# Layer 0 of a four-layer network: the placing of a batch drawn together within the next attention, and four of nine expert weight pairs asked for at the end of the last attention

## The reference, cut to what matters

```python
# attention of layer 0: 16 heads of width 16, keys and values from ctx_1024
scores = jnp.einsum('bhqd,bhkd->bhqk', Q, K) / math.sqrt(DK)
scores = jnp.where(m == 0, jnp.float32(-1000000000.0), scores)
out = jnp.einsum('bhqk,bhkd->bhqd', jax.nn.softmax(scores, axis=-1), V)
...
# experts of layer 0: 64 experts, 8 for each token, 64 slots in each expert
probs = jax.nn.softmax(logits, axis=-1)
topk_p, topk_i = jax.lax.top_k(probs, TOP_K)
flat_e = topk_i.reshape(-1)
pos_all = jnp.cumsum(jax.nn.one_hot(flat_e, NUM_EXPERTS, dtype=jnp.int32), axis=0) - 1
pos = jnp.take_along_axis(pos_all, flat_e[:, None], axis=1)[:, 0]
dispatch = dispatch.at[flat_e, pos].set(x_rep, mode='drop')
g = jax.nn.silu(jnp.einsum('ech,eih->eci', dispatch, w_gate))
u = jnp.einsum('ech,eih->eci', dispatch, w_up)
y = jnp.einsum('eci,ehi->ech', g * u, w_down)
```

## Time and profile before

| what | value |
|---|---|
| median of 3 runs | 3057.17 us (3050.08 to 3061.91) |
| the profiled execution's own time | 3043.72 us |
| its span | 3042.0 us |
| granted TensorE clock over the span | 0.904 of full speed |
| PE, DVE, ACT, POOL busy | 82%, 60%, 38%, 26% of the span |
| instructions | 35373 |

### The profile page before, as it was taken

The page is one execution under the profiler, slowest core; times in us unless marked ns, Lnnn a source line. Parts: engine busy times, 40 slices in busy tenths (PEclk is TensorE's granted clock), DMA queues, the critical chain, the costliest instruction groups (busy, mean ns, idle before and its releaser), DMA issues. The chain is left out here.

```text
span 3042.0 us, 35373 instructions
## 1 busy us (share of the span) xinstructions
PE 2490.5 (82%) x12480; PEld 1337.2 (44%) x12480; DVE 1813.2 (60%) x4051; ACT 1169.4 (38%) x2095; POOL 788.1 (26%) x494
## 2 busy tenths in 40 slices
PE   6885865086687969979989988989998998997996
PEld 2332322032354534545554454555464555454554
DVE  5673742214787747357758447776736775835775
ACT  1432331022232415245635325654415653513662
POOL 1004124462000014114414204432303442401441
PEclk8997976588587879989999999999998999998998
DMA  7411000787420020034440024432012443002442
GB/s 230 121 35 16 15 14 14 220 258 253 153 76 7 8 98 1 8 108 114 106 109 29 8 85 104 113 97 75 8 70 77 118 111 97 1 19 90 114 119 75
DMA packets 113983, 257.07 MB, mean 85 GB/s; under 512 B 37222, under 2 KB 57318, under 8 KB 107786
## 3 DMA queue, kind: packets, MB, share of 16 engines
q1 hardware_dynamic: 93978, 220.26, 24.3%
q10 hardware_dynamic: 12656, 25.97, 3.4%
q0 software_dynamic: 7168, 8.50, 1.0%
HBM read 119.81 MB, written 29.74 MB: 49 GB/s over the span
## 5 line engine op out<-in xcount | busy, mean ns | idle before, releaser
L856 POOL TENSOR_SCALAR pbuf<-pbuf,recip 128x1024 f32<-128x1024 f32 x128 | 364.4, 2847 | 946.9 <-DVE recip L760 946.9
L805 ACT ACTIVATE pbuf<-ps,least 128x1024 f32<-128x1024 f32 x256 | 284.1, 1112 | 297.9 <-DVE least L753 215.4
L753 DVE CUSTOM_DVE_ANT_0 ps<-ps,mask 128x1024 f32<-128x1024 f32 x256 | 308.0, 1244 | 143.4 <-PE ps L685 142.3
L582 POOL TENSOR_SCALAR pbuf<-pbuf,recip 128x512 f32<-128x512 f32 x128 | 200.1, 1574 | 463.5 <-DVE recip L503 463.5
L685 PE MATMUL ps<-kH,qT 64*128 64x512 f32 x1024 | 267.3, 642 | 51.2 <-ACT pbuf L805 48.4
L710 PE MATMUL ps<-work,vh 128*64 128x256 f32 x2048 | 251.8, 390 | 0.0
L553 ACT ACTIVATE pbuf<-ps,least 128x512 f32<-128x512 f32 x256 | 172.5, 685 | 159.1 <-DVE least L493 159.1
L767 DVE STREAM_TRANSPOSE pbuf<-pbuf 128x2048 f32<-128x2048 f32 (+1 forms) x128 | 226.3, 1768 | 0.8 <-issue 0.8
L1501 ACT ACTIVATE early<-ps 128x1536 f32<-128x1536 f32 x86 | 123.9, 1440 | 258.2 <-PE ps L1334 196.6
L1574 DVE TENSOR_REDUCE mh<-ps 128x3 f32<-128x1536 f32 x86 | 150.0, 1744 | 104.0 <-PE ps L1323 59.6
L990 POOL DMA_INDIRECT slot_token<-info,place x128 | 127.1, 993 | 242.1 <-DVE info L1739 193.8
(11 more groups left out here) (343 smaller groups left out, 4073.7 us busy)
## 6 DMA issues: line engine op xcount, KB each, us to landing
work<-pbuf SPq DMA_DIRECT2D x784, 96.0 KB, 2.5
work<-pbuf ACTq DMA_DIRECT2D x240, 96.0 KB, 2.9
early<-in_L_wgu SPq DMA_DIRECT2D x22, 768.0 KB
expert_rows<-zero_rows SPq DMA_DIRECT2D x16, 1024.0 KB, 11.5
yg<-expert_rows SPq DMA_DIRECT2D x16, 1024.0 KB, 5.9
early<-in_L_wd SPq DMA_DIRECT2D x22, 384.0 KB
arena<-in_L_wo SPq DMA_DIRECT2D x8, 1024.0 KB, 9.0
arena<-in_L_wff SPq DMA_DIRECT2D x4, 2048.0 KB, 9.3
```

What stands on the lines that cost most here:

```text
L582: nc.gpsimd.tensor_scalar(x, x, recip[:, n % 8:n % 8 + 1], None, mult).then_inc(probs_ready[1], 1)
L753: nc.vector.tensor_tensor_reduce(out=x, in0=x, in1=mask, scale=1.0, scalar=FMAX, op0=add, op1=ALU.min, accum_out=least[:, n % 8:n % 8 + 1])\
L805: nc.scalar.activation(to, x, ACT.Exp, bias=least[:, n % 8:n % 8 + 1], scale=-1.0, accum_out=sums[:, n % 8:n % 8 + 1]).then_inc(taken, 1)
L856: nc.gpsimd.tensor_scalar(unit(n), unit(n), recip[:, n % 8:n % 8 + 1], None, mult).then_inc(pool_divided, 1)
```

## The change

It does three things. (1) The numbers at which the pieces of a batch's routing stand are drawn closer: from base + 31.6 to 48.8 before to base + 31.6 to 43.85; GpSimd's `hand_out`, which issues a burst, goes from base + 53 to base + 43. (2) SyncE issues the weights of four pairs (`AT_ONCE`) as soon as the attention's last product is made, ahead of the last batch's rows, and the other five when the last batch is placed. (3) A wait on `normed` is put ahead of the reciprocal in `divide`, for the instruction that read the same buffer before. No operation is added or left out otherwise.

```diff
+AT_ONCE = 4
...
-                at["back", b, i] = t + 31.6 + i
-                at["project", b, i] = t + 33.6 + i
-                at["rows", b, i] = t + 38.6 + i
-            at["logits", b, 0] = t + 40.6
-            at["place", b, 0] = t + 43.6
+                at["back", b, i] = t + 31.6 + 0.7 * i
+                at["project", b, i] = t + 33.1 + 0.7 * i
+                at["rows", b, i] = t + 37.4 + 0.6 * i
+            at["logits", b, 0] = t + 38.7
+            at["place", b, 0] = t + 40.7
...
+                    if b == B - 1:
+                        sp.wait_ge(av_done, BLOCKS // 4)
+                        for i in range(AT_ONCE):
+                            load_pair(sp, a, pair_weights(early, i), i, early_in[i])
                     sp.wait_ge(x1n_ready, b + 1)
...
-                sp.wait_ge(av_done, BLOCKS // 4)
                 sp.wait_ge(placed, 2 * B - 1)
-                for i in range(EARLY):
+                for i in range(AT_ONCE, EARLY):
                     load_pair(sp, a, pair_weights(early, i), i, early_in[i])
...
                 def hand_out(b):
-                    yield base[b] + 53
+                    yield base[b] + 43
...
+                        if b or g:
+                            v.wait_ge(normed, b * QUADS + g)
                         link(nc.vector.reciprocal(r16[:, :, :], o[:, :, :, DK0]))
...
                     for n, last in enumerate(layernorm_steps(nc, link, x1, x1n, stats)):
-                        yield t0 + 35.45 + n * 0.5
+                        yield t0 + 34.3 + n * 0.2
...
-                        yield t0 + 46.3 + 1.5 * half
+                        yield t0 + 42.1 + 1.05 * half
...
-                        yield t0 + 46.8 + 1.5 * half
+                        yield t0 + 42.45 + 1.05 * half
...
-                        yield t0 + 47.3 + 1.5 * half
+                        yield t0 + 42.8 + 1.05 * half
                         nc.vector.tensor_reduce(w8[:, some, :], junk[:, some], AX.X, add).then_inc(placed, 1)
```

More of the change, by code:

```diff
@@ L1532, in routed @@
                 def routed(b):
-                    yield base[b] + 41.6
+                    yield base[b] + 39.4
                     act.wait_ge(chosen, b + 1)
@@ L1676, in route @@
                     nc.vector.tensor_scalar(negm[:, :], m8[:, :, 0], -1.0, None, mult).then_inc(chosen, 1)
-                    yield t0 + 41.3
+                    yield t0 + 39.3
                     v.wait_ge(chosen, b + 1)
@@ L1681, in route @@
                     link(last)
-                    yield t0 + 41.9
+                    yield t0 + 39.6
                     link(nc.vector.tensor_tensor(sel[:, :, :], rep[:, :, :], lg[:, :, :], ALU.not_equal))
-                    yield t0 + 42.5
+                    yield t0 + 39.9
                     for t in range(NT):
@@ L1698, in route @@
                     last.then_inc(job_kept, 1)
-                    yield t0 + 44.3
+                    yield t0 + 41.2
                     nc.vector.tensor_copy(before[:, 0, :], before[:, NT, :])
@@ L1707, in route @@
                     link(last)
-                    yield t0 + 44.9
+                    yield t0 + 41.5
                     nc.vector.tensor_tensor(ex[:, :, :], ex[:, :, :], valid[:, :, :], mult)
                     link(nc.vector.tensor_tensor(key[:, :, :], key[:, :, :], valid[:, :, :], mult))
-                    yield t0 + 45.5
+                    yield t0 + 41.8
                     for t in range(NT):
```

## The result

The changed kernel takes 3081.45 us (median of 5 runs, 3075.54 to 3083.83) where the kernel before, on the same chip, takes 3054.91 (5 runs, 3050.08 to 3061.91). The ratio is 1.0076, with a 95% interval of 1.0052 to 1.0100. It is slower, by some 23 us. The forecast was +9 and 3066, so the time lies inside the range, on the side that had a chance of 0.31.

A forecast was written before the change was run, and what follows sets the result against it. Layer 0 was held bound by the attention's 3.0 us steps (VectorE search plus wait) and by scatter bursts stopping it, burst 4 being itself the path; +8 + 9 - 8 = +9 us on 3057.17 gave 3066, range 3034 to 3088.

The forecast's parts named there:

- the side that had a chance of 0.31: Whole kernel: slower than before by over 0.5%, meaning above 3072 us; chance 0.31.
- The slower rival: Attention: TensorE's jobs in bank 7 wait on VectorE's copies behind searches; +20, +11 and -4, 3084 us; chance 0.25.
- Drawn together, +8.: Routing of batches 0 to 2 in attention: same VectorE work meets fewer free gaps; +8 us, ends -10 and +20.
- Batch 1's thirteen steps above 60 us: Batch 1's routing in the attention: 50.6 us before; above 60 us would show the forecast wrong.
- Burst 3 moved, +9.: Burst 3 goes from the tail onto attention steps: costs 27 us instead of 17.5; +9 us, bounds 0 and +11.
- Bursts 1 and 2: 0.: Both bursts move 4.5 steps earlier and stay over attention, stopping the same kind of work; 0 us.
- The early weights, -8.: Burst 4 and start of experts: fewer weight loads beside the burst shorten its waits; -8 us, ends -4 and -14.
- of the others I take half of 6.9: Burst 4's other waits, among them 2.75 and 6.9 us: half of 6.9 us counted as saved.
- The tail is freed: End of attention: burst 3 costs little over the last steps and the tail's 17.5 us go; 3029 us; chance 0.20.
- Bursts do not stop engines: Bursts: another thing causes the still part, so moving burst 3 changes nothing; +8 + 0 - 8, 3057 us; chance 0.11.
- The moved bias add: GpSimd's last bias add waits up to 41 us longer behind burst 1, its reader over 200 us on; cost 0.
- the added wait on `normed`: Ahead of each reciprocal, for an instruction already behind VectorE in its own order; cost 0.

The follow-up runs named there:

- e_paced: The changed kernel with every second scatter of bursts 1 and 2 waiting for the exponents to go on; 3016.23 us, 0.9902 of before.
- e_last_two: The kernel before with the changed kernel's numbers for batches 2 and 3 alone, weights as before; 3065.41 us, 1.0067 of before.
- e_weights: The kernel before with the early weights alone, all numbers of the order as before; 3029.12 us, 0.9938 of before.
- e_after_again: The changed kernel run once more, unchanged, where the kernel before takes 3048.34 us; 3073.84 us, 1.0087 of before.
- e_eights: The changed kernel with bursts 1 and 2 cut into runs of eight scatters, five steps apart, on the second chip; 2979.22 us, 1.0091 of before.

## Why the prediction was right in sign and short in size

The measured time lies in the forecast's range, but its mechanism did not put it there. The three terms came to +25, +11 and -5 us in the trace where the forecast had +8, +9 and -8. The time lies at the edge of what the forecast calls its own bounds, -3 and +25 us (3082), which don't follow from the ends of its terms: these add up to -24 and +27. The slower rival stretched the range to 3088.

- **"Drawn together, +8."** This is the step that failed: the term of the sum with a cost left out. It measured +25.1 us in the trace, and +29.2 on the chip without the standstill, above even its own upper end of +20. The step counted lost gaps of 1.25 us on VectorE and took each step as the sum of its work. By the rows, what it left out is that work in one piece delays the search, that TensorE idles for it (4.56 us), and that it then runs at half speed for 9 us; 20.7 of the 25.1 us lie in the steps where that happens. That the clock, and not the drawing of the norm as such, makes them long was not tested. "No compute instruction is added", and still TensorE is busy 36.7 us instead of 28.9 in those eight steps, for 15 instructions more.
- **"Batch 1's thirteen steps above 60 us"** was named as what would prove it wrong, and so it was: without a standstill in them (`e_paced`) they take 67.7 us, where before's took 50.6.
- **"Burst 3 moved, +9."** Right in mechanism and close in size: +29.9 inside for -18.5 in the tail, 11.4 net, just above its upper bound of +11; 9.3 net in `e_last_two`. The forecast put 27 against 17.5. It began at 494.66, and less the 4.2 and 25.1 us of delay that is 465, where the forecast had it.
- **"Bursts 1 and 2: 0."** Roughly so. Compared with the spaced kernels of the second chip, the steps to exponent 49 from 38 cost 32.4 us more before and 25.0 in the changed kernel, those to exponent 70 from 57 30.8 and 34.3. That is 31 to 32 us a burst before, where the forecast had 28, and 4 us less together now; neither moved by over 8.
- **"The early weights, -8."** -5.0 in the changed kernel, inside its bounds. The term named its parts, and one of two came. SyncE's read now starts 1.2 us behind the last scatter instead of 6.9 (644.50 and 643.28). The other half of the gain, "of the others I take half of 6.9", didn't come; POOL's waits of the earlier trace rows are 7.87 and 3.11 us now:

```profile
621.61 0.98 POOL L991 DMA_INDIRECT slot_token<-info,place  x1 [7.87 <-issue]
...
633.37 0.97 POOL L991 DMA_INDIRECT slot_token<-info,place  x1 [3.11 <-DMA slot_token<-info,place]
```

  Over all runs that first wait was 6.6 to 6.9 us with nine pairs asked for at once, and 5.2 to 7.9 with four of them asked for early. The stretch from burst 4 to the first gather was 55.7 us in `e_weights` and 54.6 in `e_after_again`, so the term is -5 to -7. The rule weighed in the forecast (the Trainium skill, Runtime: NRT & Kernel Launch, Instruction fetch mechanics: a branch outside the loaded window forces a fetch) would have given -4.4, nearer to the -5.0. The runs agree with it in that the wait stays, but don't show that it is a fetch.
- **The slower rival**, +20, +11 and -4 for 3084, had nearly the right numbers (25, 11, -5) with another mechanism. It had TensorE's jobs wait on each other in bank 7. The rows show TensorE waiting for the search instead, and then its clock. Waits for a job's copy are there too, but small: 0.79 us in batch 1's eight steps, 1.03 and 0.78 in batch 2's. That its sum of +27 came near was luck.
- **"The tail is freed"** (3029) fell: inside the attention the standstill cost its full price.
- **"Bursts do not stop engines"** (3057) fell on the three chips with the standstill. On the second chip its premise holds but not its time: there the changed kernel in runs of eight still takes 27 us more than before (`e_eights`). The Trainium skill (SBUF — State Buffer, Who interferes with whom) says that DMA never contends with a compute engine. The traces of the second chip agree. On the others waits of 22 to 25 us stand beside the bursts, and the runs don't show whether that is contention with DMA or arises on another path.
- The moved bias add and the added wait on `normed` were costed at nothing; no row speaks against it, and neither was tried alone.

## What to carry to other kernels

When work is packed more densely on an engine, look for the longest piece that now stands unbroken ahead of what another engine waits for, not at the sum; here 5.5 us of norm in one piece went with 8.1 us of delay, by the rows because TensorE waited for what stood behind it and its clock then fell. On a chip with the standstill, long rows of indirect DMAs from GpSimd are better spread in pairs, paced by a semaphore of the loop beside them: that took 2.2% off this one (0.9721 against 0.9938 with the early weights alone). And measure a gain on more than one chip before you call it general: the same edit was worth 80 us on one and 6 on another.

## What was not expected of the hardware

- On three chips of four, while GpSimd issues indirect DMAs without a pause, signals that VectorE and ScalarE wait for come up to 25 us late, from about 13 us into the row until its end. On the other (the second) the same instructions at the same rate (32 in 40.55 us) delay nobody. On which path the signals are held up stays open; it isn't the writing of the records, nor the number of scatters.
- The clock of TensorE, 1.00 before, stood at 0.50 for 9 us behind a wait of 4.6 us, while the engine was busy all the time. By this row, a wait costs about twice its length in such a place.
- Parts of the change measured alone gave -18, +11 and +19 us, +12 together, and the whole +23 to +27. About half of the difference lies in the tail: a part's gain can lie in what another part removes.
